# Top-2 experts: where their first weights, first gather and the reload of the residual are issued, and how two routers compute logits and the two best experts

## The chip, the cores and the metric

The kernel runs on one core of a Trainium2 chip. The metric is the device time of one execution in microseconds (us). The engines are called as in the profile: PE (matrix multiplies), PEld (its weight loads), DVE (vector), ACT (scalar), POOL (GpSimd), SP (the engine that issues most transfers).

## The reference, cut to what matters

The model has four layers of attention and feed-forward on 2048 tokens of 256 features. The change touches the feed-forward of layer 1 (each token goes to its two best of eight experts), the attention block of layer 2, and the router of the feed-forward of layer 2 (each expert takes its 1024 best tokens).

```python
x = x + _L1_ffn_ref(_layernorm(x, axis=-1), L1_ffn_router_w, L1_ffn_w1, L1_ffn_w2)
x = x + _L2_xattn_ref(_layernorm(x, axis=-1), ctx_1024, ...)
x = x + _L2_ffn_ref(_layernorm(x, axis=-1), L2_ffn_wg, ...)
# _L1_ffn_ref:
logits = jnp.einsum('bsd,ed->bse', x, router_w)
probs = jax.nn.softmax(logits, axis=-1)
topk_vals, topk_idx = jax.lax.top_k(probs, K)          # K = 2 of E = 8
for eid in range(e):
    w = jnp.sum(jnp.where(idx == eid, vals, jnp.zeros((), x.dtype)), axis=-1)
    h = jax.nn.gelu(x_flat @ w1[eid].T, approximate=False)
    y = h @ w2[eid].T
    out = out + w[:, None] * y
# _L2_xattn_ref: self attention, context attention, feed-forward, each with a layernorm
# _L2_ffn_ref:
scores = jax.nn.softmax(xt @ wg, axis=-1)
top_scores, sel = jax.lax.top_k(scores.T, CAPACITY)
```

## The kernel before, in words

The program is a row of stages; each is written in a block of code for every engine, and all engines meet at a block's end before the next block starts. Within a block each engine runs its instructions in the order of the code, and semaphores order the engines among each other. The residual `k.x` (128 partitions x 16 token tiles x 256) stays on the chip from stage to stage.

`top2_experts` has two blocks. The first is `dispatch_to_tiles`, the routing. DVE normalises the 16 token tiles into `h` (L1471). PE turns them (`turn`, L1432), ACT copies four tiles at a time to `hT` (L1419), and PE multiplies token by token: `hT` is the stationary operand and the router's eight columns `rw` are the moving one, 32 multiplies of 8 columns (L1447). A multiply of plain f32 stands in the trace as two records (64 here); turning a tile is one. From the logits DVE makes the softmax and the rank of every expert of every token by comparing all 8 x 8 pairs (L1498 to L1506), and takes ranks below 2 (L1508, L1509, `picked_ready`). PE counts the choices by multiplies with triangles of ones (L1452, L1454). DVE works out which expert each of 23 tiles of 256 slots belongs to (`experts`, L1533, `experts_ready`) and which slot each of the 4096 token-expert pairs has. For the 32 groups of pairs it writes `value` (L1558, L1562, L1565) and `lane` (L1571), and 32 multiplies over them (64 records, L1461) give every slot's token. DVE turns that into `index` (L1582, `index_ready`). So that the clock of PE stays up, filler multiplies stand in its queue (`keep_busy`, L1339): 12 at the start, 28 after the logits, 44 after the counts. SP stores `k.x` to `total` and `h` to `rows` in DRAM.

The second block works through the 23 tiles. SP loads each tile's expert weights (`w1_in`, `w2_in`, 1 MB each, L1166 and L1171), POOL gathers the 256 rows of a tile with two indirect transfers (`gather`, L1184) and adds the results to `total` with two more (`add`, L1194). ACT rounds weights and rows to a high part (L1272, L1276, L1266), DVE computes the low parts (L1303, L1308, L1298), and PE multiplies in three terms (L736 to L738) in the order `turn(0)`, `turn(1)`, `layer1(0)`, `layer1(1)`, `turn(2)`, `layer2(0)` and so on. When all additions have landed, SP reloads `k.x` from `total` with one transfer of 2 MB (L1175), and the block ends when it has landed.

`transformer_block` follows. It works on units of two token tiles (DUO); DVE's first instructions are the statistics of `k.x` (`first_moments`, L2004). At the end of each unit POOL scales the last normalisation (L1989), adds `beta3` to the unit's rows of `k.x` (L1990) and adds the two (L1992, `x_added`); DVE then takes the rows' statistics for the next stage (L2086).

`choose_tokens` is the second router. Its logits are computed as in the first (L2246, L2233, L2261); then come the softmax (L2311 on) and a search for each expert's threshold in 15 steps.

## Time and profile before

| | |
|---|---|
| time, median of 3 runs | 1747.47 us (1746.74 to 1753.26) |
| the profiled execution's own time | 1749.65 us |
| its span in the trace | 1747.8 us |
| PE busy / DVE / ACT / POOL | 1461.9 / 1106.4 / 747.3 / 641.1 us |
| granted clock of PE, mean | 0.908 of full speed |
| routing block of the top-2 experts | 452.9 to about 504 us |
| tiles of the top-2 experts | 505.2 to about 819 us |
| layer 2 attention block | 819.9 to about 1107 us |
| second router | from 1108 us |

A stage's place is read from the timeline. The clock of PE has two levels: 1.00 in the views is 2.4 GHz, 0.50 is 1.2 GHz. An engine's share of the whole span says little about one stage: in the stretches below PE waits for transfers or for DVE although it is busy for 84% of the span.

### The profile page before, as it was taken

To read this page: it belongs to the slowest core of one execution; us is meant where nothing else is said; L and a number is where in the kernel's file an instruction comes from. 1 tells how busy PE (TensorE), PEld (TensorE's weight loads), DVE (VectorE), ACT (ScalarE), POOL (GpSimd) and SP (SyncE) were. 2 spreads that over 40 slices of the span, in tenths; PEclk is the share of its full clock that TensorE was granted. 3 is DMA by queue.
4 is the path that set the end of the run, shared out by engine and by line. 5 is a ranking of instruction groups with operands and counts; after the bars stand their busy time and mean duration, and the time that the engine had idled before them with its cause. 6 is when DMAs were issued, how large, how long until landed. Compare 5 with 4: busy or idle time off the path is not lost. (4 is left out here: it accounts for less than half of the span.)

```text
span 1747.8 us, 25282 instructions
## 1 busy us (share of the span) xinstructions
PE 1461.9 (84%) x9442; PEld 1234.9 (71%) x9442; DVE 1106.4 (63%) x2427; ACT 747.3 (43%) x1285; POOL 641.1 (37%) x436
## 2 busy tenths in 40 slices
PE   7998859998868999994798997656999999599854
PEld 5786658887658999994577775425887888568722
DVE  6675767886546767772656454475676675467578
ACT  2454534443116667661435433102334443044465
POOL 1452125566013556542122222104556555235200
PEclk9898889999869999997799998677999999699978
DMA  5000000000345777754100000404444433500001
GB/s 182 1 1 5 1 1 1 1 1 1 111 149 181 216 216 228 221 160 82 59 1 1 1 1 1 134 4 155 85 98 93 99 85 49 114 1 1 1 0 49
DMA packets 94064, 122.02 MB, mean 70 GB/s; under 512 B 12188, under 2 KB 79159, under 8 KB 93943
## 3 DMA queue, kind: packets, MB, share of 16 engines
q1 hardware_dynamic: 72823, 91.56, 16.3%
q0 software_dynamic: 21120, 28.85, 9.1%
q8 instruction: 76, 1.25, 0.3%
q14 instruction: 45, 0.37, 0.1%
HBM read 94.95 MB, written 25.43 MB: 69 GB/s over the span
## 5 line engine op out<-in xcount | busy, mean ns | idle before, releaser
L2480 POOL DMA_INDIRECT ch_total<-ch_y,ch_index x64 | 107.4, 1678 | 123.8 <-DVE ch_y L2663 108.8
L1194 POOL DMA_INDIRECT t_total<-t_y,t_index x46 | 100.0, 2175 | 138.6 <-DVE t_y L1315 128.6
L3466 POOL TENSOR_TENSOR L_s<-L_s,L_mx 128x1232 f32<-128x1232 f32 x32 | 76.5, 2389 | 141.9 <-DVE L_mx L3545 141.9
L736 PE MATMUL t_ps<-t_hT_hi,t_w_hi 128*128 128x256 f32 x368 | 106.8, 290 | 7.6 <-DVE t_w_lo L1303 6.0
L736 PE MATMUL ch_ps<-ch_hT_hi,ch_w_hi 128*128 128x512 f32 x256 | 104.7, 409 | 9.7 <-DVE ch_hid L2689 6.3
L2600 ACT ACTIVATE ch_silu<-ch_ps 128x512 f32<-128x512 f32 x64 | 38.3, 599 | 172.8 <-PE ch_ps L738 170.7
L736 PE MATMUL t_ps<-t_w_hi,t_act_hi 128*128 128x256 f32 x368 | 105.8, 288 | 0.0
L737 PE MATMUL t_ps<-t_hT_lo,t_w_hi 128*128 128x256 f32 x368 | 105.6, 287 | 0.0
L738 PE MATMUL t_ps<-t_hT_hi,t_w_lo 128*128 128x256 f32 x368 | 105.6, 287 | 0.0
L738 PE MATMUL t_ps<-t_w_hi,t_act_lo 128*128 128x256 f32 x368 | 104.1, 283 | 0.0
L737 PE MATMUL t_ps<-t_w_lo,t_act_hi 128*128 128x256 f32 x368 | 104.1, 283 | 0.0
L737 PE MATMUL ch_ps<-ch_hT_lo,ch_w_hi 128*128 128x512 f32 x256 | 103.2, 403 | 0.0
L738 PE MATMUL ch_ps<-ch_hT_hi,ch_w_lo 128*128 128x512 f32 x256 | 103.0, 402 | 0.0
L2689 DVE TENSOR_TENSOR ch_hid<-ch_silu,ch_ps 128x512 f32<-128x512 f32 x64 | 43.6, 686 | 82.3 <-ACT ch_silu L2600 67.5
L3331 PEld LDWEIGHTS L_ps<-L_vb,L_pT 128*128 128x128 f32 (+1 forms) x640 | 76.0, 196 | 15.8 <-ACT L_pT L3443 15.8
L3331 PE MATMUL L_ps<-L_vb,L_pT 128*128 128x51 f32 (+2 forms) x640 | 79.7, 282 | 8.0 <-ACT L_pT L3443 8.0
L2470 POOL DMA_INDIRECT ch_hg<-ch_rows,ch_index x64 | 70.7, 1105 | 31.6 <-issue 18.9
L417 PE MATMUL L_ps<-wk_vw,L_pT 128*128 128x256 f32 (+1 forms) x320 | 73.9, 387 | 7.6 <-DVE x L626 5.3
L1327 DVE TENSOR_TENSOR t_act_lo<-t_whole,t_act_hi 128x512 fp32r<-128x512 f32 x92 | 61.7, 689 | 26.0 <-ACT t_whole L1289 23.2
L736 PEld LDWEIGHTS t_ps<-t_hT_hi,t_w_hi 128*128 128x128 f32 x368 | 72.2, 196 | 8.2 <-issue 6.2
L3537 DVE TENSOR_TENSOR L_s<-L_ps,L_neg 128x616 f32<-128x616 f32 x64 | 48.1, 794 | 45.2 <-PE L_ps L3311 45.2
L548 POOL TENSOR_TENSOR L_s<-L_s,wk_kb 128x1232 f32<-128x1232 f32 x16 | 45.2, 2823 | 78.1 <-DVE L_s L610 78.1
(518 smaller groups left out, 4447.6 us busy)
## 6 DMA issues: line engine op xcount, KB each, us to landing
t_w_in<-in_L_ffn_w1T SPq DMA_DIRECT2D x23, 1024.0 KB, 4.9
t_w_in<-in_L_ffn_w2T SPq DMA_DIRECT2D x23, 1024.0 KB, 5.6
ch_w_in<-in_L_ffn_w SPq DMA_DIRECT2D x24, 512.0 KB, 3.7
x<-in_x SPq DMA_DIRECT2D x4, 512.0 KB, 5.0
t_total<-x SPq DMA_DIRECT2D x1, 2048.0 KB
t_rows<-t2d_h SPq DMA_DIRECT2D x1, 2048.0 KB
x<-t_total SPq DMA_DIRECT2D x1, 2048.0 KB, 8.1
tb_w<-in_L_xattn_w SPq DMA_DIRECT2D x2, 1024.0 KB, 9.7
```

The lines of the kernel that those rows point to most:

```text
L417: ins = nc.tensor.matmul(ps[:, 7, 0:D], pT[0:rows, n % 2, f, :], vw[0:rows, b, f, :], start=(f == 0), stop=(f == FC - 1))
L548: nc.gpsimd.tensor_tensor(flat, flat, kb[:, n // BT, :], ALU.add).then_inc(biased, 1)
L736: nc.tensor.matmul(out, sh, mh, start=start, stop=False)
L737: nc.tensor.matmul(out, sh, ml, start=False, stop=False)
L738: return nc.tensor.matmul(out, sl, mh, start=False, stop=stop)
L1194: nc.gpsimd.indirect_dma_start(out=total, out_offset=bass.IndirectOffsetOnAxis(ap=index[:, 2 * j + u:2 * j + u + 1], axis=0), in_=y[:, j % ...
L1327: nc.vector.tensor_tensor(act_lo[:, j % 2, 2 * q:2 * q + 2, :], whole[:, q % 2], act_hi[:, j % 2, 2 * q:2 * q + 2, :].bitcast(F32), ALU.su ...
L2470: nc.gpsimd.indirect_dma_start(out=hg[:, s % 3, u, :], out_offset=None, in_=rows, in_offset=at(s, u)).then_inc(gathered[s % 3], 16)
L2480: nc.gpsimd.indirect_dma_start(out=total, out_offset=at(s, u), in_=y[:, s % 2, u, :], in_offset=None, compute_op=ALU.add).then_inc(added[s ...
L3331: ins = nc.tensor.matmul(ps_o()[:, h0 * HEAD:h1 * HEAD], pT[0:rows, n % 2, f, :], vb[0:rows, b, f, 0:(h1 - h0) * HEAD], start=(f == 0), st ...
L3466: nc.gpsimd.tensor_tensor(s[:, n % G], s[:, n % G], spread(mx[:, n % G, :], 2, [P, H, KEYS]), ALU.subtract).then_inc(shifted, 1)
L3537: nc.vector.tensor_tensor(s[:, n % G, c * 8:(c + 1) * 8, :].rearrange("p (j i) n -> p j i n", i=2), ps[:, 0:BANDS, c * 2 * KEYS:(c + 1) * ...
```

## The change

The two block boundaries and both routers are edited:

- SP issues the weights of tiles 0 and 1 in the routing block, after `experts_ready`; POOL issues the gather of tile 0 there too, after `index_ready`. The buffer `hg` and the semaphores move out for that.
- The reload of `k.x` is cut in eight transfers of two tiles; the expert block doesn't wait for them, but `first_moments` waits for its own two (`k.x_back`). These four semaphores live as long as the program and are cleared at its end.
- Both routers multiply with the router's eight columns stationary and 512 tokens moving (`by_expert`), ACT copies the 8 x 512 result, and PE turns it back in four pieces of 128 (`by_token`).
- The two best experts are found by two rounds of a maximum with ties broken by the lowest expert (`best`), instead of the 64 pairs.
- `value` is made in four parts, each just before or after its part of `lane`.
- In the attention block POOL adds `beta3` before it waits for the last normalisation.

```diff
+        hg = sb("hg", [P, 3, 2, D])
...
+        def load_weights(sp, j):
+            e = sp.value_load(experts[0:1, j:j + 1], min_val=0, max_val=E - 1)
+            if j >= 2:
+                sp.wait_ge(w1_hi_ready, j - 1)
+                sp.wait_ge(w1_lo_ready, j - 1)
+            sp.dma_start(w1_in[:, j % 2], i["L1_ffn_w1T"][bass.ds(e, 1)].rearrange("o (c p) j -> p (o c) j", p=P)
+                         ).then_inc(w1_loaded[j % 2], 16)
...
+        def gather_rows(j):
+            for u in range(2):
+                nc.gpsimd.indirect_dma_start(
+                    out=hg[:, j % 3, u, :], out_offset=None, in_=rows,
+                    in_offset=bass.IndirectOffsetOnAxis(ap=index[:, 2 * j + u:2 * j + u + 1], axis=0)
+                ).then_inc(gathered[j % 3], 16)
...
-            sp.wait_ge(experts_ready, 1)
-            for j in range(TILES):
...
+            for j in range(2, TILES):
+                load_weights(sp, j)
             for n in range(2):
                 sp.wait_ge(added[n], 32 * len(range(n, TILES, 2)))
-            sp.dma_start(k.x[:], total[0:T, :].rearrange("(t p) d -> p t d", p=P)).then_inc(restored, 16)
-            sp.wait_ge(restored, 16)
+            for m in range(BT // DUO):
+                for b in range(B):
+                    ts = slice(b * BT + m * DUO, b * BT + (m + 1) * DUO)
+                    sp.dma_start(k.x[:, ts, :], total[0:T, :].rearrange("(t p) d -> p t d", p=P)[:, ts, :]
+                                 ).then_inc(k.x_back[m], 16)
...
-            pool.wait_ge(rows_stored, 64)
-            pool.wait_ge(index_ready, 1)
-            for j in range(3):
-                gather(j)
+            gather(1)
+            gather(2)
...
+            sp.wait_ge(experts_ready, 1)
+            for j in range(2):
+                load_weights(sp, j)
             sp.wait_ge(rows_stored, 64)
...
+            pool.wait_ge(rows_stored, 64)
+            pool.wait_ge(index_ready, 1)
+            gather_rows(0)
...
+            def logits_copied(g):
+                act.wait_ge(expert_psum, g + 1)
+                if g >= 2:
+                    act.wait_ge(logits_psum, g - 1)
+                nc.scalar.copy(of_expert[:, g % 2, :], ps[0:E, 5 + g % 2, :]).then_inc(expert_rows, 1)
...
+            def by_expert(g):
                 pe.wait_ge(hT_ready, g + 1)
+                if g >= 2:
+                    pe.wait_ge(expert_rows, g - 1)
+                for kc in range(KC):
+                    ins = nc.tensor.matmul(ps[0:E, 5 + g % 2, :], rw[:, kc, :], hT[:, g % 2, kc, :],
+                                           start=(kc == 0), stop=(kc == KC - 1))
+                ins.then_inc(expert_psum, 1)
+
+            def by_token(g):
+                pe.wait_ge(expert_rows, g + 1)
                 for u in range(G):
                     t = g * G + u
-                    for kc in range(KC):
-                        ins = nc.tensor.matmul(ps_l[:, t * E:(t + 1) * E], hT[:, g % 2, kc, u * P:(u + 1) * P],
-                                               rw[:, kc, :], start=(kc == 0), stop=(kc == KC - 1))
-            ins.then_inc(logits_psum, 1)
+                    ins = nc.tensor.transpose(ps_l[:, t * E:(t + 1) * E], of_expert[:, g % 2, u * P:(u + 1) * P],
+                                              k.ident[0:E, 0:E])
+                ins.then_inc(logits_psum, 1)
+
+            for g in range(NG):
+                by_expert(g)
+                if g + 2 < NG:
+                    turn(g + 2)
+                if g:
+                    by_token(g - 1)
+            by_token(NG - 1)
             keep_busy(nc, ps[:, 7, :], filler, 28)
...
+            def best(values, mine):
+                order = spread(earlier[:], 1, wide)
+                chain(nc.vector.tensor_reduce(mx[:], values[:], AX.X, ALU.max))
+                chain.wait()
+                chain(nc.vector.tensor_tensor(equal[:], values[:], spread(mx[:], 2, wide), ALU.is_equal))
+                chain.wait()
+                chain(nc.vector.tensor_tensor(equal[:], equal[:], order, ALU.mult))
+                chain.wait()
+                chain(nc.vector.tensor_reduce(mx[:], equal[:], AX.X, ALU.max))
+                chain.wait()
+                chain(nc.vector.tensor_tensor(mine[:], spread(mx[:], 2, wide), order, ALU.is_equal))
+                chain.wait()
...
             part = PAIRS // PARTS
+            vs = [P, part, SLOTS]
             for q in range(PARTS):
...
+                chain(nc.vector.tensor_tensor(value[:, ms, 1, :], spread(places[:], 1, vs), spread(hi[:, ms], 2, vs),
+                                              ALU.is_equal))
                 nc.vector.tensor_tensor(lane[:, ms, :], spread(lanes[:], 1, [P, part, P]), spread(lo[:, ms], 2, [P, part, P]),
                                         ALU.is_equal).then_inc(lane_ready, 1)
+                chain.wait()
+                chain(nc.vector.tensor_tensor(value[:, ms, 0, :], value[:, ms, 1, :], spread(token[:, ts], 2, vs), ALU.mult))
+                chain.wait()
+                nc.vector.tensor_tensor(value[:, ms, 1, :], value[:, ms, 1, :],
+                                        spread(gate[:].rearrange("p v t -> p (v t)")[:, ms], 2, vs), ALU.mult
+                                        ).then_inc(value_ready, 1)
...
+                    pool.wait_ge(rows_ready[0], DUO * g + DUO)
+                    chain(nc.gpsimd.tensor_tensor(own, own, spread(affine[:, 6, :], 1, [P, DUO, D]), ALU.add))
                     pool.wait_ge(rows_ready[3], DUO * g + DUO)
                     chain(nc.gpsimd.tensor_tensor(n3[:, g % 2], n3[:, g % 2], spread(affine[:, 5, :], 1, [P, DUO, D]), ALU.mult))
-                    chain(nc.gpsimd.tensor_tensor(own, own, spread(affine[:, 6, :], 1, [P, DUO, D]), ALU.add))
...
             def first_moments(n):
                 rows = [k.x[:, unit(a)[0] * BT + unit(a)[1] + u, :] for a in (2 * n - 2, 2 * n - 1) for u in range(DUO)]
+                dve.wait_ge(k.x_back[n - 1], 16 * B)
...
+        handed = Semaphores(nc, ctx, "handed_")
+        k.x_back = [handed(f"x_back{m}") for m in range(BT // DUO)]
```

PE's queue in the first routing block, before: after the turned tiles (`t_ps<-ident,t2d_h`) stand the multiplies of 8 columns, then the fillers.

```order
L1432 MATMUL t_ps<-ident,t2d_h 128x128 x16
L1447 MATMUL t_ps<-t2d_rw,t2d_hT 128x8 x8
L1432 MATMUL t_ps<-ident,t2d_h 128x128 x8
L1447 MATMUL t_ps<-t2d_rw,t2d_hT 128x8 x8
L1432 MATMUL t_ps<-ident,t2d_h 128x128 x8
L1447 MATMUL t_ps<-t2d_rw,t2d_hT 128x8 x16
L1339 MATMUL t_ps<-t2d_filler 128x512 x28
```

The same place of PE in the changed kernel (`t2d_of_expert` is the 8 x 512 result that is turned back; the shapes are the output's partitions and columns).

```order
L1459 MATMUL t_ps<-ident,t2d_h 128x128 x16
L1473 MATMUL t_ps<-t2d_hT,t2d_rw 8x512 x2
L1459 MATMUL t_ps<-ident,t2d_h 128x128 x8
L1473 MATMUL t_ps<-t2d_hT,t2d_rw 8x512 x2
L1459 MATMUL t_ps<-ident,t2d_h 128x128 x8
L1481 MATMUL t_ps<-ident,t2d_of_expert 128x8 x4
L1473 MATMUL t_ps<-t2d_hT,t2d_rw 8x512 x2
L1481 MATMUL t_ps<-ident,t2d_of_expert 128x8 x4
L1473 MATMUL t_ps<-t2d_hT,t2d_rw 8x512 x2
L1481 MATMUL t_ps<-ident,t2d_of_expert 128x8 x8
L1345 MATMUL t_ps<-t2d_filler 128x512 x28
```

The 32 multiplies of 8 columns became 8 multiplies of 512 columns and 16 turns of an 8 x 128 piece; the number of fillers is the same.

POOL's queue around the boundary of the two blocks (the branches are the end of one block and the start of the next), before:

```order
L1412 IOTA t2d_spare 128x46
L1382 UNCONDITIONAL_BRANCH
L1178 UNCONDITIONAL_BRANCH
L1184 DMA t_hg<-t_rows,t_index 128x256 x8
L1194 DMA t_total<-t_y,t_index 2304x256 x2
```

and in the changed kernel:

```order
L1425 IOTA t2d_spare 128x46
L1144 DMA t_hg<-t_rows,t_index 128x256 x2
L1390 UNCONDITIONAL_BRANCH
L1190 UNCONDITIONAL_BRANCH
L1144 DMA t_hg<-t_rows,t_index 128x256 x6
L1202 DMA t_total<-t_y,t_index 2304x256 x2
```

Two of the eight gathers that stood behind the boundary now stand ahead of it, so all engines pass the boundary after them. SP's four transfers of the first weights moved past it in the same way.

## Rows read from the trace of the kernel before

**Rows 1.** Timeline, first router on PE: start, us, engine, line, operation

```profile
459.86 1.95 PE L1447 MATMUL t_ps<-t2d_rw,t2d_hT 128*128 128x8 f32 x16
...
465.19 3.96 PE L1447 MATMUL t_ps<-t2d_rw,t2d_hT 128*128 128x8 f32 x32
```

**Rows 2.** Timeline, choice of the two best, and two dependent DVE operations

```profile
471.11 1.22 DVE L1498 TENSOR_TENSOR t2d_same<-t2d_probs 128x1024 f32<-128x1024 f32 x1
...
477.75 0.23 PE L1452 MATMUL t_ps<-t2d_picked,t2d_before_b 128*128 128x136 bf16 x1 [1.21 <-DVEq L1511]
...
481.21 0.29 DVE L1538 TENSOR_TENSOR t2d_slot<-t2d_slot,t2d_sel 128x128 f32<-128x128 f32 x1
481.54 0.28 DVE L1540 TENSOR_REDUCE t2d_pair<-t2d_slot 128x16 f32<-128x128 f32 x1
```

**Rows 3.** Timeline, the two later runs of fillers on PE

```profile
469.00 7.55 PE L1339 MATMUL t_ps<-t2d_filler 128*128 128x512 bf16 x28
...
478.38 9.66 PE L1339 MATMUL t_ps<-t2d_filler 128*128 128x512 bf16 x44
```

**Rows 4.** Timeline, `value`, `lane` and their multiplies

```profile
484.06 1.69 DVE L1558 TENSOR_TENSOR t2d_value<-t2d_places,t2d_hi 128x1472 f32<-128x1472 f32 x1
...
489.31 4.63 DVE L1571 TENSOR_TENSOR t2d_lane<-t2d_lanes,t2d_lo 128x1024 f32<-128x1024 f32 x4
...
490.59 12.49 PE L1461 MATMUL t_ps<-t2d_value,t2d_lane 128*128 128x92 f32 x64 [2.55 <-DVE t2d_lane L1571]
```

**Rows 5.** Windows: stretch, us, busy us of each engine, granted clock, DMA

```profile
492.00:494.00 2.00, 2.00 (x13) 2.00 (x13) 1.94 (x2) 0.00 (x0) 0.00 (x0) 0.56 0.00 0
...
1120.00:1122.00 2.00, 2.00 (x13) 2.00 (x13) 0.00 (x0) 0.00 (x0) 0.00 (x0) 0.57 1.01 325
```

**Rows 6.** Timeline, from the last index to the first tile's multiplies

```profile
503.71 0.19 DVE L1582 TENSOR_SCALAR t_index<-t2d_found 128x46 int32<-128x46 f32 x1
505.18 1.30 POOL L1184 DMA_INDIRECT t_hg<-t_rows,t_index  x1 [50.43 <-issue]
...
510.67 1.90 ACT L1272 CAST t_w_hi<-t_w_in 128x2048 fp32r<-128x2048 f32 x1 [40.53 <-DMA t_w_in<-in_L_ffn_w1T]
...
512.60 2.29 DVE L1303 TENSOR_TENSOR t_w_lo<-t_w_in,t_w_hi 128x2048 fp32r<-128x2048 f32 x1 [8.70 <-ACT t_w_hi L1272]
...
513.08 1.12 PE L1216 MATMUL t_ps<-ident,t_hg 128*128 128x128 f32 x4 [10.00 <-DMA t_hg<-t_rows,t_index]
...
518.73 0.58 PE L736 MATMUL t_ps<-t_hT_hi,t_w_hi 128*128 128x256 f32 x1 [1.59 <-DVE t_hT_lo L1298]
```

**Rows 7.** Timeline, from the reload to the attention block

```profile
810.62 0.37 SPq L1175 DMA_DIRECT2D x<-t_total  x1
...
819.92 1.40 DVE L2004 BATCH_NORM_STATS2 tb_st<-x 128x6 f32<-128x256 f32 x4 [15.89 <-PEq L729]
```

**Rows 8.** Second router's logits: ns min/median/max, first and last start

```profile
L2261 PE MATMUL ch_ps<-ct_rw,ct_hT x64: 175/266/361, 1115.8 to 1128.3; 128*128 128x8 f32 x64
```

**Rows 9.** Timeline, f32 multiplies of 512 columns; a copy of 512 values

```profile
38.82 3.70 PE L3299 MATMUL L_ps<-L_hT,L_wq_sb 128*128 128x512 f32 x8 [0.37 <-ACT L_hT L3398]
...
444.12 0.59 ACT L520 COPY L_pT<-L_ps 128x512 f32<-128x512 f32 x1 [6.86 <-PE L_ps L406]
```

**Rows 10.** The page's part on issues: KB each, us to landing

```profile
t_w_in<-in_L_ffn_w1T SPq DMA_DIRECT2D x23, 1024.0 KB, 4.9
```

**Rows 11.** Timeline of POOL and DVE in the tile loop; landing of the gathers

```profile
549.48 2.80 POOL L1194 DMA_INDIRECT t_total<-t_y,t_index  x1 [0.30 <-issue]
...
548.55 2.29 DVE L1308 TENSOR_TENSOR t_w_lo<-t_w_in,t_w_hi 128x2048 fp32r<-128x2048 f32 x1 [1.30 <-ACT t_w_hi L1276]
...
DMA to landing us min/median/max: 3.7/4.8/6.7
```

**Rows 12.** Timeline, attention block: DVE's wait, and POOL's addition of `beta3`

```profile
963.02 0.31 DVE L2040 TENSOR_REDUCE tb_cmx<-tb_cs 128x2 f32<-128x154 f32 x1 [4.47 <-ACT tb_cs L1900]
...
1103.60 1.26 POOL L1990 TENSOR_TENSOR x<-x,tb_affine 128x512 f32<-128x512 f32 x1
```

137 lines of the change are left out of this document (69 added, 68 removed).

## The prediction

> **What bounds the kernel now.** I read the timeline first, at the block boundaries and in both routers, and then the windows for the clock. PE is the busy engine over the whole span, but every stretch the change touches is one where PE waits or turns fillers, so its 84% decides nothing there.
>
> In the first router PE multiplies for logits from 459.86 and ends at 465.19 + 3.96 = 469.15, some 9.3 us: 64 records at 0.12 each [rows 1], the rest turns of the last two groups. DVE then needs from 471.11 to 477.75 for the choice [rows 2]; the fillers beside it hide [rows 3]. From 484.06 to 489.31 DVE makes `value` whole, then the four parts of `lane`; PE starts at 490.59 and needs 12.49 us, 0.195 a record [rows 4], because its clock falls to the low level of 1.2 GHz (0.56 in that window, the fall lying in it) [rows 5]. The index is there at 503.90. All engines pass the boundary, POOL issues at 505.18, ACT waits for weights until 510.67, PE for gathered rows until 513.08, and the first multiply of the first tile starts at 518.73, 14.8 us after the index [rows 6]. At the other end SP issues the reload at 810.62 and DVE starts the next stage at 819.92, 9.3 us later [rows 7]; nobody works. The second router's logits take from 1115.8 to about 1128.6, 12.8 us, longer than the first's 9.3, since there the clock falls soon after 1120 (0.57 from 1120 to 1122) [rows 5, 8]. Between these places the 23 tiles and the attention units run at PE's pace and take over any earlier start whole.
>
> **The sum, term by term** (plus is time won).
>
> *Logits, first router, and the choice: +0.6.* The multiply turned round looks as if it removed work: 8 for 32. But a plain f32 multiply is two records, and one of 512 columns costs (3.70 - 0.6)/7 = 0.44 at the high clock, 0.6 being about the length of one by itself [rows 9]. So 16 x 0.44 = 7.0 stand against 64 x 0.12 = 7.7 [rows 1]. The 16 pieces turned back come on top; no row shows an 8 x 128 piece, so I bound it from below by nothing and from above by the 0.12 of [rows 1], its nearest row (128 columns of stationary operand, 8 moving), and take that: 1.9. The last group can't overlap its copy: 0.59 [rows 9] and some 0.3 until a result is seen, less the 0.45 of turning the group before, 0.45 of waiting. Together 9.4 against 7.7: logits come 1.7 to 1.8 later. ACT's other copies lie beside PE's work; if that cover were gone they would cost 0.6 each, three times. The choice becomes eleven dependent operations on 128 values at 0.33 each (from 481.21 to 481.54 in [rows 2]) and two more of about 0.5 together, 4.2 with the hand-over, against 6.6: 2.4 won. Net 0.6. The 28 fillers start 1.8 later, at 470.8; at 9.66/44 = 0.22 each [rows 3] they end at 476.9, just before PE is wanted at 477.1. Did they run as slowly as before (7.55), they would end at 478.4 and the term be -0.6. Range -0.6 to 1.5.
>
> *`value` in parts: +4.9.* A part of `value` has 368 elements. From 1.69 for 1472 and 1.14 a part for 1024 [rows 4] about 0.5 each; a part of DVE's work is 0.45 + 1.14 + 0.55 + 0.45 = 2.6. The first part is ready at 484.06 + 2.7 = 486.8. But 44 fillers stand before it and end at 478.38 + 9.66 = 488.04 [rows 3]: they are late next, and 1.2 us of the gain stays with them. The four parts are ready at 486.8, 489.4, 492.0, 494.6. With the clock up (1.9 us a part) PE ends at 496.5; at the low level throughout (3.1) at 500.5; before it was 503.1. Won: 2.6 to 6.6. In the trace the clock fell some 1.6 us into these multiplies, after 2.55 of idling [rows 4, 5]; now they follow the fillers directly. I take two parts up and two down: 488.0, 489.9, 491.9, 495.1, 498.2, so 4.9.
>
> *Weights and first gather early: +4.7.* The weights are asked for after `experts`, at about 481. A transfer of 1 MB lands 4.9 after its issue [rows 10]; even one after the other the four are there by 501, and the two of tile 0 by 491, ahead of the boundary. This part is free: SP has nothing behind them but its wait for `rows`, stored long before. The gather is not free: POOL issues both halves (1.30 for the first [rows 6], and I take 1.3 for the second with its gap) before the boundary, and everybody waits behind it. So the block opens at index + 2.6 + 1.3 = index + 3.9 instead of + 1.3. Then ACT casts at once (1.90), DVE follows (2.29), and hT's parts are ready about 5.2 after the opening. PE, however, stands at `turn(1)`, which needs gather 1, still issued after the boundary: second half at about +1.4, landing 3.7 later (the least in [rows 11]; the queues are empty now), 1.1 for the turns [rows 6]: +6.2. So the first multiply comes at index + 10.1 against 14.8. Ends: 5.6 if gather 1 doesn't hold it, 1.9 if POOL is held up (first rival).
>
> *Reload: +4.3.* An issue takes SP 0.37 [rows 7], with a gap 0.4 to 0.5; eight of them last until about 814.3. A boundary takes 1.3, as from 503.90 to 505.18 [rows 6], so DVE starts at 815.6 instead of 819.92. The 2 MB landed 1.3 before 819.92, 8.0 after their issue; a quarter of them, 512 KB, should need about half of that and is there at 815 or a little after. The later parts have units of time, and the next stage's own small loads, which queue behind them, are not what DVE starts with. Range 0 (second rival) to 4.6.
>
> *Second router: +1.8.* It has no choice of two and no late fillers, so it shows the logits alone: 9.3 + 1.75 = 11.0 against 12.8 if the clock stays up, until 1126.8. That it stays up is my choice: between the fillers of 512 columns, 0.22 each, it was at the high level all along [rows 3], and eight such multiplies now stand between the turns. If it falls at 1120 or 1121 as before, the 6.5 us left then double: -4.8. Range -4.8 to 2.0.
>
> *POOL's addition ahead: +1.2.* In the last unit `beta3`'s 1.26 lies between the scaling and the last addition [rows 12], and leaves the path. In earlier units it now falls into DVE's statistics. *Semaphores cleared at the end: -0.5*; between 0 and the 1.3 that a boundary takes.
>
> Sum 0.6 + 4.9 + 4.7 + 4.3 + 1.8 + 1.2 - 0.5 = 17.0. Against the profiled execution's own 1749.65 that is 1732.7; that execution lies 2.2 above the median shown (1747.47), so a median of 1730.5.
>
> **A rule against the change.** POOL's indirect issue of 549.48 took 2.80, and DVE's L1308 ran from 548.55 to 550.84, its usual 2.29 [rows 11]: POOL finished 1.44 after DVE's end, little more than the 1.30 of a whole issue in [rows 6], as if it had begun there. The Trainium skill, page "SBUF — State Buffer", section "SBUF: two separate sides", says that DVE and GpSimd take the port pair they share as an exclusive lock, and that an indirect transfer's descriptors can't be written while DVE holds it. The trace agrees. By that rule the early-gather term would be the first rival's 1.9 and the median 1733.3; by my reading of who comes first it is 4.7.
>
> **The rivals.**
> 1. *DVE holds POOL up in gather 1.* DVE's L1303 starts 2.0 after the opening (ACT's 1.90 [rows 6]); POOL's second half of gather 1 runs from about 1.3 to 2.2 or, if the first needs 1.30 again, from 1.6 to 2.6. If held, it ends after 4.3 + 0.8, lands 2.8 later, and the first multiply comes at index + 12.9: the term is 1.9, the median 1733.3. For it: [rows 11]. Against it: POOL is first, by a few tenths.
> 2. *The block end waits for its transfers.* No row shows a block ending with a transfer under way. Then the reload's term is nothing: 1734.8.
> 3. *The clock falls in a router.* Second router at -4.8: 1737.1. The first likewise would add about 4: 1741.
> 4. *Slower than before.* The low level in the tile loop: 96 multiplies a tile at 0.195 instead of 0.12 (the two levels of a small f32 multiply in [rows 1, 4]) are 7.2 us a tile. It would need 17.0 + 8.7 = 26 us lost, nearly four tiles at the low level, for a time above 1756. The loop enters with PE just idled, 10.00 before its first turns [rows 6], as it would again, after a shorter wait; so I hold it unlikely.
>
> The moved addition in earlier units is costed at nothing: the statistics it delays are followed by 4.47 us of DVE idling [rows 12]; with that cover gone it would be at most the addition's 1.26 a unit, 10 us.
>
> **How the numbers follow.** Forecast, 14 to 21 won, 1726.5 to 1733.5: 0.55. Rival 1: 0.18. Rival 2: 0.07. Rival 3: 0.13, of which 0.03 reaches down to no change. Two rivals together or the cover gone, 3 to 9 won: 0.05. Rival 4: 0.02. What a measurement can tell from no change is about 0.5%, 8.7 us, that is below 1738.7: faster 0.90, same 0.08, slower 0.02. The range leaves out 1 in 10 on the slow side and little on the fast side: 1724 (all terms near their upper ends, 22 to 23 won) to 1739 (rival 3, or 1 with 2).
>
> **What the changed profile would show.** Per record 0.44 for the 512-column multiplies and DVE's first maximum 1.7 to 1.8 later than before; PE wanted at the counts at about 477; the multiplies for the slots right behind the fillers, in steps of 2.6; POOL's first two gathers ahead of the boundary and the opening 3.9 after the index, the first tile's multiply 6.2 after that, its wait ended by the gather and not by weights; DVE's statistics 5 after SP's first reload. What would make it wrong: 512-column multiplies with 8 outputs costing other than 0.44, a boundary longer than 1.3 with POOL's transfers under way, or the level of the clock.

## The result, and the profile after

| | before | changed |
|---|---|---|
| median of 6 runs each, side by side | 1749.01 us (1746.74 to 1753.26) | 1734.26 us (1727.82 to 1738.93) |
| ratio, 95% interval | | 0.9916 (0.9894 to 0.9938) |
| the profiled execution: time, span | 1749.65, 1747.8 us | 1732.91, 1731.1 us |
| granted clock, mean | 0.908 | 0.923 |

The kernel became 14.75 us (0.84%) faster; the forecast was 17.0 and 1730.5, the range 1724 to 1739. A second measurement of the same changed kernel, below, gave 1735.60 and 0.9940 (0.9920 to 0.9961), with medians 8.7 apart. Every ratio in this document is against the kernel before, run side by side with it.

The profile after, where [rows 1] to [rows 8] were read before. PE's timeline in the first router (start, us, engine, line, operation, number of records, wait in brackets):

```profile
456.91 1.88 PE L1473 MATMUL t_ps<-t2d_hT,t2d_rw 128*8 128x512 f32 x4
...
462.59 0.41 PE L1481 MATMUL t_ps<-ident,t2d_of_expert 8*128 8x8 f32 x4
...
467.63 0.41 PE L1481 MATMUL t_ps<-ident,t2d_of_expert 8*128 8x8 f32 x4 [0.32 <-ACT t2d_of_expert L1437]
468.20 5.99 PE L1345 MATMUL t_ps<-t2d_filler 128*128 128x512 bf16 x27 [0.16 <-issue]
474.17 0.23 PE L1494 MATMUL t_ps<-t2d_picked,t2d_before_b 128*128 128x136 bf16 x1
```

Four records of 512 columns take 1.88 together and start 0.43 apart; a piece turned back costs about 0.1. The stage's blocks begin at 449.82 (452.86 before), so DVE's first maximum at 468.08 stands 18.26 after the start against 16.32: 1.94 later. The counts at 474.17 stand 24.35 against 24.89: 0.54 won.

The same timeline at the multiplies for the slots; DVE's parts begin at 480.41, 483.04, 485.65 and 488.27:

```profile
484.30 3.70 PE L1504 MATMUL t_ps<-t2d_value,t2d_lane 128*128 128x92 f32 x32
488.50 1.99 PE L1504 MATMUL t_ps<-t2d_value,t2d_lane 128*128 128x92 f32 x16 [0.50 <-DVE t2d_value L1615]
491.12 1.99 PE L1504 MATMUL t_ps<-t2d_value,t2d_lane 128*128 128x92 f32 x16 [0.62 <-DVE t2d_value L1615]
```

In the last row of [rows 4] these took 12.49; now 8.81 pass from first to last, at the high level (0.12 a record), and PE waits for DVE's `value` (L1615), not for fillers. The fillers are 1.2 us late for the first part and some 0.4 for the second; for the third and fourth they no longer matter.

From the last index to the first tile, timeline of all engines:

```profile
493.74 0.19 DVE L1627 TENSOR_SCALAR t_index<-t2d_found 128x46 int32<-128x46 f32 x1
494.93 1.29 POOL L1144 DMA_INDIRECT t_hg<-t_rows,t_index  x1 [43.14 <-DVEq L1630]
496.52 0.96 POOL L1144 DMA_INDIRECT t_hg<-t_rows,t_index  x1 [0.30 <-issue]
499.64 1.09 PE L1222 MATMUL t_ps<-ident,t_hg 128*128 128x128 f32 x4 [6.53 <-PEq L1390]
499.67 1.90 ACT L1278 CAST t_w_hi<-t_w_in 128x2048 fp32r<-128x2048 f32 x1 [30.63 <-PEq L1390]
500.24 0.94 POOL L1144 DMA_INDIRECT t_hg<-t_rows,t_index  x1 [2.76 <-POOLq L1390]
501.48 0.95 POOL L1144 DMA_INDIRECT t_hg<-t_rows,t_index  x1 [0.30 <-issue]
501.60 2.29 DVE L1309 TENSOR_TENSOR t_w_lo<-t_w_in,t_w_hi 128x2048 fp32r<-128x2048 f32 x1 [7.67 <-ACT t_w_hi L1278]
504.22 1.12 PE L1222 MATMUL t_ps<-ident,t_hg 128*128 128x128 f32 x4 [3.50 <-DMA t_hg<-t_rows,t_index]
504.99 0.56 PE L736 MATMUL t_ps<-t_hT_hi,t_w_hi 128*128 128x256 f32 x1
```

ACT and PE are let go at 499.6, 5.7 after the index, by the block's end (`PEq L1390`), 2.1 after POOL's last issue. What ends it stands among the instructions of that end, which the view of one line lists (duration in ns, then the start):

```profile
L1390 POOLq DRAIN  x1: 4213/4213/4213, 495.1 to 495.1; - x1
L1390 ACTq EVENT_SEMAPHORE  x1: 17/17/17, 499.5 to 499.5; - x1
```

POOL's drain (the instruction with which an engine ends its part of a block) lasts until 499.36, and the second half of the gather had landed at 499.23. In experiments 4, 7, 9 and 11, with the same gather ahead of the boundary, it ends 0.13 after that landing as well. The first multiply follows 11.06 after the index (14.83 before).

The other end, in the timeline:

```profile
797.17 3.96 SPq L1187 DMA_DIRECT2D x<-t_total  x8
...
802.28 1.41 DVE L2050 BATCH_NORM_STATS2 tb_st<-x 128x6 f32<-128x256 f32 x4 [11.64 <-PEq L729]
```

and in the view of the line that ends the expert block:

```profile
L1109 POOLq DRAIN  x1: 9142/9142/9142, 791.7 to 791.7; - x1
L1109 SPq DRAIN  x1: 122/122/122, 801.2 to 801.2; - x1
```

DVE starts 5.11 after the first reload issue (9.30 in [rows 7]), and no longer waits for the residual. POOL's drain is over at 800.8, just before SP's, which begins when the eighth issue is over and ends at 801.3. The second router's multiplies of 512 columns run at the high level throughout (windows: stretch, us, busy of PE, PEld, DVE, ACT, POOL, granted clock, DMA):

```profile
1094.00:1108.00 14.00, 13.51 (x68) 5.96 (x65) 5.70 (x27) 6.34 (x8) 0.00 (x0) 1.00 1.04 332
1108.00:1110.00 2.00, 0.09 (x1) 0.12 (x2) 1.29 (x5) 0.31 (x1) 0.00 (x0) 1.00 0.61 215
```

**Where the time came from.** Both traces cut at the same events, by the rows' starts, the last index and `x_added` by the rows' ends; the last two columns are a second profile of each kernel, taken with the experiments:

| stretch, us | before | changed | before again | changed again |
|---|---|---|---|---|
| ahead of the routing block | 452.86 | 449.82 | 446.73 | 453.19 |
| logits: start to first maximum | 16.32 | 18.26 | 22.25 | 18.26 |
| choice: to the counts | 8.57 | 6.09 | 8.56 | 6.10 |
| counts to last index | 26.15 | 19.76 | 21.04 | 19.74 |
| last index to first tile's multiply | 14.83 | 11.06 | 14.72 | 11.04 |
| tiles: to POOL's last addition issue | 288.06 | 288.39 | 287.62 | 288.40 |
| to the first reload issue | 3.83 | 3.79 | 3.76 | 3.76 |
| reload issue to DVE's statistics | 9.30 | 5.11 | 9.49 | 5.11 |
| attention block, to `x_added` | 286.28 | 285.62 | 288.81 | 285.67 |
| second router, to its threshold search | 24.56 | 22.01 | 21.45 | 22.02 |
| threshold search | 30.81 | 30.53 | 30.81 | 30.53 |
| **sum of the stretches the change can reach** | **708.71** | **690.62** | **708.51** | **690.63** |
| the rest, to the span's end | 586.2 | 590.7 | 590.0 | 594.5 |

The stretches that the change can reach became 18.1 and 17.9 us shorter, and their sum repeats to 0.2. In the changed kernel the single ones repeat too, to 0.1. In the kernel before they don't: the logits differ by 5.9, the counts to the index by 5.1, the attention block by 2.5 and the second router by 3.1, and the sums agree because these cancel. The stretches that it can't reach, ahead and behind, differ from one execution to the next with no edit in them: over the fourteen profiles of this study the one ahead takes 440.9 to 453.2 us, the one behind 581 to 598. That is why the whole times scatter by 11 us and why the ratio, not the table, has the wide interval.

### The profile page after: what moved, and what is told of

The parts are those of the page before. It is cut to its first block and busy times, and to the rows that moved or that the text cites. A ratio compares the mean times of both kernels' runs of the same rounds, so it can differ in the third digit from the quotient of the medians.

```text
span 1731.1 us, 25203 instructions
## 1 busy us (share of the span) xinstructions
PE 1444.6 (83%) x9368; PEld 1209.6 (70%) x9378; DVE 1110.9 (64%) x2441; ACT 751.1 (43%) x1293; POOL 641.2 (37%) x437
## 3 DMA queue, kind: packets, MB, share of 16 engines
q1 hardware_dynamic: 72935, 91.56, 16.5%
```

## The experiments

Each is the changed kernel with one edit, unless said otherwise. Differences of whole times under some 4 to 6 us can't be told apart (each ratio's interval is 0.4 to 0.7% wide), so each is read in its own stretch first. The second router takes 22.0 us in six of the ten profiles with the changed form and 23.4 in the other four, whatever the edit; a sum that has this 1.4 in it is named. The sum is that of the table above, 690.6 for the changed kernel.

**1. The gather of tile 0 behind the boundary.**

```diff
-            pool.wait_ge(rows_stored, 64)
-            pool.wait_ge(index_ready, 1)
-            gather_rows(0)
...
-            gather(1)
-            gather(2)
+            pool.wait_ge(index_ready, 1)
+            for j in range(3):
+                gather(j)
```

> The changed kernel with the gather of tile 0 put back behind the boundary; the early weights stay. Read in the stretch from the last index to the first tile's first multiply, which took 14.8 us before and takes 11.1 in the changed kernel. Theory (the early gather earns its place, because POOL's issues behind the boundary meet DVE's low parts): the boundary opens 1.3 after the index, two issues of 1.3 and 1.0 put tile 0's rows at about index + 7.3, but the two issues for tile 1 fall into DVE's L1309 and finish after it, so tile 1's rows land at index + 10.5 or later and the first multiply comes at index + 12 to 13: 1 to 2 us slower than the changed kernel. Rival (the boundary, 5.7 us with the gather ahead of it, takes back what the gather gives): the first multiply comes at index + 10.5 to 11.3, no slower, and the early weights alone are the whole gain of this place.

Measured: index to first multiply 12.73 (11.06 changed, 14.83 before); sum 692.7, of which 1.4 is the second router's; 1737.36 us, 0.9951 (0.9931 to 0.9970). The boundary was passed at once (ACT works 0.5 after the index) and DVE's low part came in POOL's way, though in tile 0's second half instead of tile 1's. POOL, then DVE:

```profile
494.85 1.29 POOL L1144 DMA_INDIRECT t_hg<-t_rows,t_index  x1 [43.35 <-POOLq L1391]
496.44 2.74 POOL L1144 DMA_INDIRECT t_hg<-t_rows,t_index  x1 [0.30 <-issue]
499.49 0.95 POOL L1144 DMA_INDIRECT t_hg<-t_rows,t_index  x1 [0.30 <-issue]
...
496.06 2.29 DVE L1310 TENSOR_TENSOR t_w_lo<-t_w_in,t_w_hi 128x2048 fp32r<-128x2048 f32 x1 [2.42 <-ACT t_w_hi L1279]
```

So of the 3.77 us won at this place the early gather gives 1.67 and the early weights 2.1. The theory's size was right; the place where POOL is held was not. Two thirds of the 1.67 come back behind it, though: the tile loop takes 287.28 instead of 288.39. More on this stands below the experiments.

**2. `value` whole again.**

```diff
-            for q in range(PARTS):
-                ...
-                chain(nc.vector.tensor_tensor(value[:, ms, 1, :], ..., ALU.is_equal))
+            chain(nc.vector.tensor_tensor(value[:, :, 1, :], spread(places[:], 1, vs), spread(hi[:], 2, vs), ALU.is_equal))
...
-                pe.wait_ge(value_ready, q + 1)
```

> The changed kernel with value made whole before the four parts of lane, as before. Read from the counts (the first multiply with triangles) to the last index. Theory (most of the 6.4 us won there is the clock and not the order): PE idles about 2.5 us again, the clock falls, the 64 records take 12 us and more, and the last index comes 6.4 later against the counts; time 6 to 7 us above the changed kernel. Rival (the order alone): the clock stays at the high level, the 64 records take about 7.5, and the index comes only 1.5 to 2 later.

Measured: counts to index 20.96 against 19.76, 1.20 longer. PE idles 2.47 as it did before the change, but the clock doesn't fall:

```profile
486.65 7.38 PE L1503 MATMUL t_ps<-t2d_value,t2d_lane 128*128 128x92 f32 x64 [2.47 <-DVE t2d_lane L1617]
```

The theory fell, the rival holds for this execution: the order gives 1.2, and 5.1 of the 6.4 were the clock's. The sum, 690.65, is that of the changed kernel all the same: the tile loop is 1.06 shorter. The median, 1738.05 (0.9958, 0.9932 to 0.9984), is 3.8 above the changed kernel's first one and 2.5 above its second; it can't be told apart from either.

**3. Both routers token by token, as before.**

```diff
-            for g in range(NG):
-                by_expert(g)
-                ...
+            for g in range(NG):
+                ...
+                    for kc in range(KC):
+                        ins = nc.tensor.matmul(ps_l[:, t * E:(t + 1) * E], hT[:, g % 2, kc, u * P:(u + 1) * P],
+                                               rw[:, kc, :], start=(kc == 0), stop=(kc == KC - 1))
```

> The changed kernel with both routers multiplying token by token again (8 columns moving), the shorter choice kept. Theory (turned round, the logits cost more in themselves and pay only where they keep the clock up): in the first router DVE's first maximum comes 1.9 us earlier after the stage's start (16.3 instead of 18.3 us); in the second router the clock falls in the last multiplies and the turned probabilities come 2.5 later (22.7 instead of 20.1 us after the block's start); together +0.6 against the changed kernel. Rival (the clock fell there before by chance): it stays up in the second router too, the logits come about 1.8 earlier in both, and the kernel is 3.7 us faster than the changed one.

Measured: first maximum 16.48 (1.78 earlier, as expected); from there to the counts 7.16 instead of 6.09, because the fillers end at 472.6: they start after the logits as before, but 27 of them take 7.13 instead of 5.99. So 0.71 is won up to the counts. The granted clock tells why the fillers are slow; the first line is this run's, the second the same place in the kernel before:

```profile
464.00:466.00 2.00, 1.77 (x11) 1.45 (x12) 0.58 (x2) 0.05 (x1) 0.00 (x0) 0.59 0.65 212
468.00:470.00 2.00, 2.00 (x11) 1.41 (x11) 0.58 (x2) 0.17 (x1) 0.00 (x0) 0.59 0.79 261
```

 The second router's logits and softmax take 0.44 less than with the wide form, not 2.5 more. Median 1729.38 (0.9914, 0.9881 to 0.9947). Neither theory was right whole: in both routers the clock fell as the last multiplies of 8 columns ended, too late to cost the logits much. The sum is 687.5, 3.1 below the changed kernel and the lowest of all; 2.1 of that is a tile loop of 286.31, in which nothing was edited. So in this execution the old form was the faster one.

**4. The reload as one transfer of 2 MB, not waited for in the block.**

```diff
-            for m in range(BT // DUO):
-                for b in range(B):
-                    ...
+            sp.dma_start(k.x[:], total[0:T, :].rearrange("(t p) d -> p t d", p=P)).then_inc(k.x_back[0], 16)
...
-                dve.wait_ge(k.x_back[n - 1], 16 * B)
+                dve.wait_ge(k.x_back[0], 16)
```

> The changed kernel with the residual reloaded by one transfer of 2 MB, as before, but the expert block doesn't wait for it: DVE's first statistics do. It parts the gain of 4.2 us at this place into pieces and boundary. Theory (the pieces count, the boundary lies beside the transfer): the 2 MB land 8.0 after their issue and DVE starts then, 8.0 to 8.2 after the issue, against 5.1 with eight pieces and 9.3 before: 3.0 slower than the changed kernel. Rival A (a block that ends with a transfer under way waits for it at its end): 9.3, 4.2 slower. Rival B (the transfer alone lands in 5 us when nothing else waits): 5.1 or less, no slower.

Measured: DVE starts 8.24 after the issue, as the theory has it, 3.13 more than with pieces; median 1735.18 (0.9939, 0.9918 to 0.9959).

```profile
807.66 1.40 DVE L2046 BATCH_NORM_STATS2 tb_st<-x 128x6 f32<-128x256 f32 x4 [14.75 <-DMA x<-t_total]
```

So the pieces give 3.1 of this place's 4.2 and the boundary beside the transfer 1.1. The sum is 694.1. The next block's first instruction of SP came 4.6 after the issue, though: something other than SP held the block's end.

**5. The kernel before, with `value` in four parts and nothing else.** The edit is that part of the change's diff, made in the kernel before.

```diff
+                pe.wait_ge(value_ready, q + 1)
...
             for q in range(PARTS):
...
+                chain(nc.vector.tensor_tensor(value[:, ms, 1, :], spread(places[:], 1, vs), spread(hi[:, ms], 2, vs),
+                                              ALU.is_equal))
```

> The kernel before with value made in four parts, and nothing else of the change. The run with value whole in the changed kernel kept the clock up and put the index only 1.2 later, against 6.4 between the two profiles. Theory A (in the kernel before, the clock falls in these multiplies in most executions; the parts keep it up): the profile shows the high level there, the counts-to-index stretch takes 19.8 instead of 26.2 us, and the median is 6 us below before, ratio 0.9963. Theory B (it fell there by chance in the one profile; the order alone pays): the stretch is the same 19.8, but the median is only 1 to 2 us below before, ratio 0.999.

Measured: counts to index 19.84 instead of 26.15, as both have it. But the logits of the first router, untouched, took 22.28 instead of 16.32: the clock fell there instead.

```profile
467.50 6.83 PE L1447 MATMUL t_ps<-t2d_rw,t2d_hT 128*128 128x8 f32 x32
```

3.96 in [rows 1]. The sum is 708.8, as in the kernel before (708.7 and 708.5), the ratio 1.0008 (0.9982 to 1.0034). Theory A (0.9963) lies outside the interval, B (0.999) inside, and no gain at all lies inside too.

**6. The first weights' halves made early.** ACT's cast of w1 of tile 0 stands behind its last exponential, DVE's low part ahead of its wait for the slots; `turn(1)` stands behind `layer1(0)`.

```diff
+        def first_lo(dve):
+            dve.wait_ge(w1_hi_ready, 1)
+            nc.vector.tensor_tensor(w1_lo[:, 0], w1_in[:, 0], w1_hi[:, 0].bitcast(F32), ALU.subtract
+                                    ).then_inc(w1_lo_ready, 1)
...
+            first_lo(dve)
             dve.wait_ge(slots_psum, 1)
...
             turn(0)
-            turn(1)
```

> The changed kernel, in which ACT makes the high part of the first weights in the routing block behind its last exponential, and DVE their low part while it waits for the multiplies for the slots; PE turns tile 1's rows after layer1(0). In the changed kernel the first tile's multiply comes 5.35 after its rows were turned; where the low part was ready already (the run with the gather behind the boundary) it came 2.52 after. Theory (nothing else stands in that place): index to first multiply 8.2 instead of 11.1 us, so 2.8 us won, and the tile loop keeps its 287 to 288 us. Rival A (DVE's 2.29 us are late for the slots): the index comes up to 1.5 later and half is lost. Rival B (the tile loop takes it back, since tile 1's rows or the second weights' parts are late next): the loop is 2 to 3 us longer and nothing is won.

Measured: index to first multiply 8.28 instead of 11.06, the index not later, the tiles 287.90. DVE's low part fills its idle time exactly:

```profile
489.68 2.28 DVE L1132 TENSOR_TENSOR t_w_lo<-t_w_in,t_w_hi 128x2048 fp32r<-128x2048 f32 x1
491.94 0.21 DVE L1630 SCALAR_TENSOR_TENSOR t2d_found<-t_ps,t2d_spare 128x46 f32<-128x46 f32 x1
```

The theory holds, 2.8 us. Sum 689.0, in spite of the second router's 1.4; 1728.22 us, 0.9897 (0.9871 to 0.9923).

**7. Only the first two pieces of the reload in the expert block, six behind it.**

```diff
+            k.reload = reload
+            reload(sp, 0)
...
+            for m in range(1, BT // DUO):
+                k.reload(sp, m)
```

> The changed kernel, in which SP issues only the first two of the eight pieces of the reload in the expert block and the other six first thing in the attention block. Theory (the eight issues are what the block's end waits for): DVE starts when two issues and a boundary are over and the first 512 KB have landed, 3 to 3.7 after the first issue instead of 5.1: 1.5 to 2 us won at DVE's start. Rival A (a block that ends with a transfer under way costs 4.3 us beyond the issue, as with the one transfer of 2 MB, whose next block opened 4.6 after its issue): DVE starts 5.0 after or later, nothing won. Rival B (the attention block's own small loads, behind six issues of 0.5, are late next): DVE starts earlier, but the attention block takes as much longer.

Measured: DVE starts 4.69 after the first issue, only 0.42 earlier. Rival A's number is the nearer one, its cause is not: SP's part of the block's end was over at 789.1; POOL's drain was not.

```profile
L1109 POOLq DRAIN  x1: 9162/9162/9162, 782.6 to 782.6; - x1
L1109 SPq DRAIN  x1: 128/128/128, 789.0 to 789.0; - x1
```

It ends at 791.8, 3.7 after SP's first issue (788.08), and the block with it. The 0.42 won are the time by which SP's eight issues ended behind POOL's drain in the changed kernel. In the run with one transfer of 2 MB it ended 3.7 after as well (794.0 + 9.15 = 803.15 against 799.42), in the changed kernel too (800.84 against 797.17). In the kernel before it lay under the reload, and could have been read there: it ends at 814.4, 3.8 after SP's issue at 810.62.

```profile
L1109 POOLq DRAIN  x1: 9266/9266/9266, 805.1 to 805.1; - x1
```

Sum 690.7; 1733.12 us, 0.9928 (0.9902 to 0.9955).

**8. POOL waits for the first gather itself.**

```diff
             gather_rows(0)
+            pool.wait_ge(gathered[0], 32)
```

> The changed kernel with an explicit wait of POOL for the landing of the first gather at the end of the routing block. The boundary opened 5.7 after the index there, 2.1 after POOL's last issue, and with no gather ahead of it 0.5. Theory (the block's end waits for POOL's transfers already, and that is the missing 1.6 us): the added wait changes little, the first turn comes 5.7 to 6.0 after the index. Rival (the boundary only happened to open then, the transfer is not waited for): the landing and a boundary of 0.5 to 1.2 add up and the first turn comes 6.3 to 7 after the index.

Measured: first turn 5.99 after the index (5.71 without the wait), and the drain shrank from 4.21 to

```profile
L1390 POOLq DRAIN  x1: 213/213/213, 494.6 to 494.6; - x1
```

So the routing block's end already waited for the landing of what POOL had issued: the theory. Sum 690.8; one run, 1735.66 us.

**9. Combined: 6 and 7, and POOL waits for its last additions.**

```diff
                 add(j)
+            for n in range(2):
+                pool.wait_ge(added[n], 32 * len(range(n, TILES, 2)))
```

> The changed kernel with the early halves of the first weights, with two of the eight reload pieces in the expert block and six behind it, and with POOL waiting for its last additions before the block's end. In the changed kernel POOL's drain at that end lasts 9.1 us and is over 3.7 after SP's first reload issue; in the routing block an explicit wait cut the drain from 4.2 to 0.2 us. Theory (the drain of POOL's own transfers is what held the next block back with two pieces, and a wait on their semaphore ends sooner than the drain): POOL's drain is short, the block opens about 2.2 after the first reload issue, and DVE starts when the first 512 KB have landed, 3.0 to 3.5 after that issue, against 5.1 in the changed kernel and 4.7 with two pieces alone. With 2.8 at the entry this makes 4.5 to 5 us, about 1729.5 where the changed kernel has 1734.3. Rival (the drain lasts until its own time whatever is waited for, since the additions in DRAM take longer than their semaphores tell): DVE starts 4.7 after, and the gain is 3.2.

Measured: index to first multiply 8.20, as expected. At the other end both theory and rival missed: DVE starts 5.69 after the first issue, 1.0 later than without the wait (experiment 7).

```profile
L1109 POOLq DRAIN  x1: 4546/4546/4546, 791.3 to 791.3; - x1
```

All additions have landed when this drain begins, and it lasts 4.55 all the same. Sum 689.2, with the second router's 1.4 in it; 1727.00 us, 0.9904 (0.9878 to 0.9931).

**10. The combined kernel with the gather of tile 0 behind the boundary.** The edit is that of experiment 1, made in the kernel of experiment 9.

```diff
-            gather_rows(0)
```

> The same with the gather of tile 0 behind the boundary again. With the low part of the first weights made early, nothing of DVE's stands beside POOL's first issues any more. Theory (the early gather paid only because POOL met DVE's L1309 behind the boundary, and with that gone it is worth nothing, since the drain for it takes what it gives): the second issue takes about 1.0 instead of 2.7, turn(0) comes 5.6 to 6.0 after the index and the first multiply 8.1 to 8.6, within 0.4 of the combined kernel. Rival (it is worth its 1.7 us in itself): the first multiply comes at index + 9.5 or later.

Measured: first multiply 9.46 after the index, 1.26 more than with the early gather: the rival. With no DVE work beside it the second issue took 0.96 (2.74 in experiment 1), as expected, but turn(0) came only 6.90 after the index:

```profile
492.47 1.29 POOL L1155 DMA_INDIRECT t_hg<-t_rows,t_index  x1 [43.38 <-POOLq L1404]
494.06 0.96 POOL L1155 DMA_INDIRECT t_hg<-t_rows,t_index  x1 [0.30 <-issue]
```

The rows landed later although they were issued as fast: 5.3 and 4.0 us after the two issues began, against 3.1 and 2.7 in experiment 9, where no third gather follows until the block has ended. Sum 689.2, the same as in experiment 9: of the 1.26 the tile loop takes back 0.94 and the attention block 0.4. The medians are 7 us apart, 1733.95 (0.9942, 0.9920 to 0.9965) against 1727.00, but the two profiled executions took 1727.26 and 1727.23; the intervals just overlap, and no stretch of the table shows such a difference.

**11. The changed kernel again; 12. the kernel before again.** No edit in either.

> The changed kernel itself, as the yardstick of the two above on the same chip, and for a second profile: the logits of the first router 18.3, the multiplies for the slots 8.8, the second router 20.1 or 21.6 us; median 1734, ratio 0.992.

> The kernel before itself, for a second profile. Theory (where its clock falls in the routers and in the multiplies for the slots is chance from execution to execution): at least one of the three stretches, 16.3 for the first logits, 12.5 for the slots, 22.7 for the second router, comes out otherwise by 2 us or more. Rival (the falls belong to the kernel's own order): all three repeat within 0.3.

The changed kernel: 1735.60 us, 0.9940 (0.9920 to 0.9961), stretches in the table. The kernel before: 1747.05 us against 1744.30 beside it, 1.0012 (0.9997 to 1.0028), and in its profile the theory, three times over. Logits 22.25 (16.32), the records for the slots 7.38 (12.49), the second router's 21.45 (24.56). Its windows at the slots' multiplies:

```profile
490.00:492.00 2.00, 1.62 (x14) 1.62 (x15) 2.00 (x3) 0.00 (x0) 0.00 (x0) 1.00 0.00 0
492.00:494.00 2.00, 2.00 (x20) 2.00 (x20) 1.73 (x2) 0.00 (x0) 0.00 (x0) 1.00 0.03 8
```

and in the first profile of before:

```profile
490.00:492.00 2.00, 1.41 (x12) 1.41 (x13) 2.00 (x3) 0.00 (x0) 0.00 (x0) 1.00 0.00 0
```

From the counts up to 492 the two executions do the same, 2.55 of idling on PE and then these multiplies; one goes on at 1.00, the other falls in the next window, to a mean of 0.56 [rows 5]. Further back they differ: the second one had its low stretch in the logits.

**The entry of the tile loop, over all fourteen profiles.** PE enters the loop at the low level in each of them, after idling at the boundary. The granted clock over the loop's first 20 us and the length of the loop go together: 0.71 and 288.4 in both profiles of the changed kernel, 0.74 and 287.3 in experiment 2, 0.75 and 287.3 in experiment 1, 0.76 and 286.9 in experiment 10, 0.78 and 286.3 in experiment 3. Where the loop began later, as in experiments 1, 2 and 10, the clock was back up sooner after its start, and most of what the edit had cost ahead of the loop was given back. That the clock is the cause is argued from these numbers; no run changed it alone.

## Why the prediction was right, point by point

The sum of terms for the stretches, 17.5 without the clearing at the end, stands against 18.1 in the first pair of profiles. That this is so close is luck in part. Three of its steps were wrong: the two on the clock, where the falls of one execution were taken for the kernel's, in place and time, and the opening of the second block. The time alone wouldn't have told: 1734.26 lies nearer to rival 1 (1733.3) and rival 2 (1734.8) than to 1730.5, and only the stretches rule them out.

- *Logits and choice, +0.6*: 0.54. Logits 1.94 later (1.7 to 1.8), choice 2.48 shorter (2.4). The fillers ran at 0.22 each and ended when PE was wanted. The 7.55 of the run before, for as many fillers, came from the clock (0.59 from 468 to 470), which the prediction didn't read: "between the fillers of 512 columns, 0.22 each, it was at the high level all along [rows 3]" holds for the second run of fillers alone.
- *`value` in parts, +4.9*: between the two profiles 6.4, but the reason I gave fell. "In the trace the clock fell some 1.6 us into these multiplies, after 2.55 of idling; now they follow the fillers directly": twice the same idling of about 2.5 was not followed by a fall (experiments 2 and 12). The parts themselves give 1.2 with the clock up, and with `value` whole the tile loop gave 1.06 of that back (experiment 2). They are made at the pace I worked out (2.62 each), and what I named as late next, the fillers, holds the first two parts; for parts three and four it is DVE.
- *Weights and first gather, +4.7*: 3.77. The step that failed is the block's opening at "index + 3.9". POOL's first issue began 1.0 after the index and not at once, and the end of the block waits in POOL's drain for the gather's landing, which is over 1.88 after the last issue's end: 5.7. From there the multiply came 5.35 later (6.2 forecast, bounded by `turn(1)`); here ACT's cast, DVE's low parts and tile 1's rows end together.
- *Rival 1, DVE holds POOL up in gather 1*: it did not (0.94 and 0.95); it held up gather 2 (1.98 and 2.58, each ended 0.82 after a DVE operation), which nobody waited for. That DVE's operation holds POOL up is now shown with and without it: 2.74 in experiment 1, ended 0.83 after DVE's, and 0.96 in experiment 10. The Trainium skill, page "SBUF — State Buffer", section "SBUF: two separate sides", has the same as an exclusive lock on a shared port pair; the trace agrees. By that rule the early gather pays by keeping POOL out of DVE's way; experiment 10 shows 1.26 of its 1.67 left when DVE isn't there at all, so most of its worth up to the first multiply is in the landing. In the sums there is little left of it: 0.6 in experiment 1, without the second router's 1.4, and nothing in experiment 10.
- *Reload, +4.3*: 4.2. *Rival 2, the block end waits for its transfers*: not for SP's. In experiment 4 the next block opened 3.6 us before SP's transfer had landed. For POOL's gathers it does, at the routing block's end. At the expert block's end POOL's drain outlasts even the landing of its additions by 3.7 us; it cost nothing here only because SP's eight issues took 0.4 longer.
- *Second router, +1.8*: 2.55 in the first pair of profiles, -0.6 in the second pair. "Longer than the first's 9.3, since there the clock falls" took the early fall of one execution for the kernel's. Where the clock stays up until the last multiplies, the wide form is the longer one: here 13.2 us from the first multiply for logits to the turned probabilities against 11.6 in the second profile of before, in the first router 1.9 in all.
- *Rival 3, the clock falls in a router*: not in any of ten profiles with the wide form, in neither router's logits (18.26 to 18.30 in the first). In the old form it fell in all four profiles, in both routers, sooner or later in the logits: in the first they took 22.3 in two and 16.3 to 16.5 in the others, in the second router the stretch was 24.6 in two and 21.5 in the others. So the wide form does keep the clock up, as the prediction chose; how early it falls in the old form is what changes from one execution to the next. The second router's 1.4 more in four of the ten lies ahead of the logits: after `x_added` the clock stayed at the low level for 8.5 us instead of 5.6, and the first multiply of 512 columns came at 10.2 instead of 8.8.
- *POOL's addition, +1.2*: 0.66 in the first pair, 3.14 in the second, where the block of the kernel before was 2.5 longer. The last unit's 1.2 is there (POOL's scaling is followed at once by the last addition, 1085.30 and 1086.64); by the first pair the units before are 0.6 longer. Whether the moved addition causes this wasn't tried.
- *The 23 tiles take over any earlier start whole*: between before and changed they do (288.06 and 288.39). By experiments 1, 2 and 10 a shift of 1 to 2 us at the entry comes through for about a third or less.
- *Semaphores at the end, -0.5*: the view of that line (L728) has eleven such clearings instead of ten, and the last ones start 0.4 to 0.6 apart.

**Why the whole came out smaller than the sum.** 18.1 and 17.9 in the stretches stand against 14.75 between the medians of the first measurement and 8.7 in the second (10.5 by its ratio). In the first pair the rest was 3.0 shorter ahead and 4.5 longer behind, of which 0.5 is the clearing; nothing else there was edited. The rest varies by more than the difference, so the gain of the stretches and the medians don't contradict each other, but two profiles of each kernel are too few to say how often the clock falls in each place. Some of the 18 is such falls: in the first profile of before they cost 5.1 at the slots and 3.1 in the second router, in the second 5.9 in the logits. Added up without them, the change's own steps give about 10: 0.5 for logits and choice, 1.2 for the order of `value`, 3.8, 4.2 and 0.7 for the addition, less 0.6 in the second router. An average gain between 10 and 18 would follow; 14.75 lies in it, 8.7 below it, though its interval reaches up to 14.0. How much an execution of before loses to such falls on average stays open.

**What beats both kernels.** The early halves (experiment 6), 2.8 us in their stretch and 0.9897 in time against 0.9916 and 0.9940; the intervals overlap, the stretch is clear. What was added to it in experiment 9 at the reload cost 0.6 there. The old form of the logits with the new choice (experiment 3) has a lower sum still, 687.5 against 689.0, in its one profile; by the two falls in four profiles of that form it can lose 6 us in the first router. The two together weren't tried.

## What to carry to other kernels

Cut the traces of before and after at the same events and compare the stretches that the edit can reach: in the changed kernel they repeated to 0.1 us here, where the whole time scattered by 11. Read their sum as well: what experiments 1, 2 and 10 lost in one stretch came back for the most part in the next. Before a clock fall seen in one profile is charged to the idle time ahead of it, take a second profile of the same kernel. The block that ended behind POOL's gathers waited in POOL's drain until they had landed, while SP's reload went on under the boundary; work that needs only loaded data (here the halves of the weights) can go into an engine's idle time ahead of the boundary.

## What the runs showed of the hardware that was not expected

- POOL's drain at a block's end: 4.21 us with two indirect gathers under way, over 0.13 after the second had landed, and 0.21 after a wait for their semaphore (experiment 8). At the end of the expert block it ended 3.7 us after the last additions' semaphores had let SP go on, whatever SP's transfers were (one of 2 MB, two or eight of 256 KB), and an explicit wait made it end later still (4.55 long, experiment 9). What it waits for there is open.
- With the same 8-column multiplies the first maximum came 16.3 or 22.3 us after the block's start from one execution to the next, at 1.00 or 0.50 granted; with 512 columns moving it repeated to 0.04 us in ten profiles. The wide form, dearer by 1.8 to 1.9 where the clock is up, is the steadier one.
- In the kernel before, two executions with falls in different places took 708.71 and 708.51 us over the same stretches.
- The tile loop, 23 tiles without an edit, took 286.3 to 288.4 us, the shorter the higher the granted clock of its first 20 us (0.78 to 0.71).
